# Row maxima in pieces, projections over 128 + 64 channels, a reordered end of each attention layer, and seven products whose results nobody reads

## The reference, cut to what matters

```python
y = layer_norm(x) * scale + bias                 # then padded to 28 x 28, windows of 14 x 14
q, k, v = split(windows(y) @ qkv_w + qkv_b)      # 12 heads of 16 channels
attn = einsum(q / 4, k) + rel_h(q) + rel_w(q)    # 196 x 196 per head and window
out = softmax(attn) @ v
x = x + unwindow(out @ proj_w + proj_b)
h = gelu(layer_norm(x) @ fc1_w + fc1_b)          # 192 -> 768
x = x + h @ fc2_w + fc2_b                        # 768 -> 192
```

## Time and profile before

| | us |
|---|---|
| median of 3 runs | 443.46 (442.67 to 444.38) |
| the profiled execution | 443.95 |
| its span, first to last instruction | 441.8 |
| TensorE busy in it | 385.9 (87%) |
| VectorE busy | 198.7 (45%) |
| ScalarE busy | 145.4 (33%) |
| GpSimd busy | 98.2 (22%) |
| mean granted TensorE clock | 0.973 |

### The profile page before, as it was taken

One profiled execution on the slowest core, in us unless ns is written; L12 is line 12 of the kernel. 1 busy time (PEld: TensorE's weight loads), 2 busy tenths in 40 slices (PEclk: granted clock), 3 DMA queues, 4 the chain that ended last, 5 costly groups with the idle time before them and its releaser, 6 DMA issues.

```text
span 441.8 us, 10357 instructions
## 1 busy us (share of the span) xinstructions
PE 385.9 (87%) x4462; PEld 279.3 (63%) x4462; DVE 198.7 (45%) x435; ACT 145.4 (33%) x314; POOL 98.2 (22%) x180
## 2 busy tenths in 40 slices
PE   5979877888776999999979987887879699999997
PEld 2468865556654447968737865555657254986657
DVE  6325555655647210225853455455555430151282
ACT  2462343343352151021156234434344034011220
POOL 2304057321225230000040407622123300000000
PEclk8899999999999799999999999999999699999999
DMA  7960000000020102000201000000000000000002
GB/s 212 274 163 5 2 2 5 2 4 2 4 83 2 45 0 56 34 20 1 71 3 25 1 4 3 4 2 3 4 3 1 1 0 1 0 1 0 0 1 71
DMA packets 8302, 12.32 MB, mean 28 GB/s; under 512 B 3041, under 2 KB 5922, under 8 KB 8258
## 3 DMA queue, kind: packets, MB, share of 16 engines
q1 hardware_dynamic: 8258, 11.68, 9.5%
HBM read 10.25 MB, written 0.79 MB: 25 GB/s over the span
## 4 chain that ended last, share of the span: by engine, by line
PE 69%; DVE 21%; ACT 5%; issue 2%; DMA 1%; SPq 1%
PE banks L824 9%; PE banks L728 9%; PE banks L833 7%; DVE negmax L1228 7%; PE banks L761 7%; PE banks L666 5%; PE banks L677 5%; DVE negmax L1232 4%; PE banks L654 3%; DVE o_turned L1247 3%; DVE inverse_sums L1253 3%; PE banks L686 3%; PE banks L748 2%; ACT o_and_sums L1063 2%; PE banks L993 2%
## 5 line engine op out<-in xcount | busy, mean ns | idle before, releaser
L1071 ACT ACTIVATE arena<-banks 128x392 f32<-128x392 f32 (+2 forms) x144 | 58.7, 494 | 71.4 <-PE banks L748 71.4
L824 PE MATMUL banks<-yT,fc 96*128 96x512 f32 x96 | 48.5, 660 | 4.7 <-ACT yT L1018 2.9
L1228 DVE TENSOR_REDUCE negmax<-banks 128x8 f32<-128x1568 f32 x24 | 42.4, 1765 | 18.5 <-PE banks L728 18.5
L606 POOL TENSOR_TENSOR attention_arena<-o_and_sums,inverse_sums 128x196 f32<-128x196 f32 (+2 forms) x36 | 19.6, 545 | 124.0 <-DVE inverse_sums L1253 124.0
L728 PE MATMUL banks<-attention_arena 32*128 32x196 f32 x384 | 28.6, 367 | 19.0 <-DVE negmax L1228 15.8
L1247 DVE STREAM_TRANSPOSE o_turned<-o_and_sums 128x224 f32<-128x224 f32 x36 | 14.8, 411 | 64.2 <-ACT o_and_sums L1063 64.1
L824 PEld LDWEIGHTS banks<-yT,fc 96*128 96x128 f32 x96 | 19.8, 213 | 29.3 <-issue 22.5
L761 PE MATMUL banks<-arena,v_and_ones 128*32 128x196 f32 (+2 forms) x672 | 30.9, 308 | 4.1 <-ACT arena L1071 4.1
L728 PEld LDWEIGHTS banks<-attention_arena 32*128 32x128 f32 x384 | 15.5, 183 | 29.3 <-DVE negmax L1228 20.2
L833 PEld LDWEIGHTS banks<-fc,arena 128*128 128x128 f32 x192 | 31.3, 190 | 1.0 <-issue 1.0
L833 PE MATMUL banks<-fc,arena 128*128 128x192 f32 x192 | 31.5, 326 | 0.0
(11 more groups left out here) (155 smaller groups left out, 636.6 us busy)
## 6 DMA issues: line engine op xcount, KB each, us to landing
fc<-in_fc SPq DMA_DIRECT2D x4, 576.0 KB, 6.2
attention_arena<-negmaxT SPq DMA_DIRECT2D x72, 1.0 KB
rel<-in_rel SPq DMA_DIRECT2D x2, 448.0 KB, 5.2
qkv<-in_qkv SPq DMA_DIRECT2D x2, 432.0 KB, 4.7
x_tok<-in_x SPq DMA_DIRECT2D x4, 192.0 KB, 3.4
inverse<-in_inverse SPq DMA_DIRECT2D x1, 768.0 KB
edge_rel<-negmaxT SPq DMA_DIRECT2D x48, 0.5 KB
inverse<-in_space_back SPq DMA_DIRECT2D x1, 768.0 KB, 4.4
```

The lines of the kernel that those rows point to most:

```text
L824: last = mm(m.bank[j % 4][:, :], wl["fc1"][:, half, 128 * hid:128 * (hid + 1)], m.yT[:, half, 512 * g:512 * (g + 1)], start=half == 0, sto ...
L1071: run(m.probsT[:, n % P_RING, j, 0:cols], m.bank[4 + j][:, 0:cols], ACT.Exp).then_inc(s.probs, 1)
L1228: dve.tensor_reduce(at[:, 0:8].rearrange("k (j a) -> k j a", a=2), m.banks[:, 0:4, 0:2 * MAIN_KEYS].rearrange("k j (a n) -> k j a n", a=2) ...
```

## The change

Line numbers of the changed kernel are higher: its `score` is L792, `turn` L812, `weigh` L825, `project` L707 and L713, values L726 and L732, `relate` L755, the products that nobody reads L740, fc1 L886, maxima L1305, ScalarE's tables L1083.

- **Layout.** `m.yT` and the weights hold channels 0 to 127 in one half and 64 to 191 in the other. A product over 192 channels is now one over 128 rows ("long") and one over 64 rows ("short"). Even jobs take the short one from partitions 64 to 127, odd jobs from 0 to 63, into different banks, and the short ones of a batch follow one another. `qkv` and `fc1` loads grow by a third.
- **Projections.** The jobs use all eight banks; v and v_edge come before rel_w and rel_h. The second `turn_norm` stands right in front of the product that waits for it. Results of the six c jobs come only after all six long products.
- **Maxima in pieces.** Each piece writes columns 0 to 195 of four banks and has its own TENSOR_REDUCE. The first five pieces alternate between banks 0 to 3 and 4 to 7, all in front of turn(0); later ones use banks 0 to 3. `AHEAD` is 2: iteration n is turn(n), the last piece of group n + 2, weigh(n - 1), the first piece of group n + 3 (edges have one piece). VectorE takes both maxima ahead of `invert(n - 1)`.
- **End.** fc1 uses eight banks in batches of four, long products first; the output of image 3 is projected between the long and the short ones of the first batch, into bank 7. ScalarE does two Gelus, loads the root's table, takes the second root, loads the Gelu table again. GpSimd's bias addition waits for six Gelus.
- **Products nobody reads.** `keep_warm` makes 128 x 512 products: 2 in front of rel_w, 3 in front of turn(0), 2 in front of the transposes of the end.

The diff, cut:

```diff
+PROJ += [("v", n, 0, "act") for n in range(IMAGES)] + [("v_edge", n, 0, "act") for n in range(2)]
 PROJ += [("rel_w", n, 0, "act") for n in range(SIDE // 2)] + [("rel_h", n, 0, "dve") for n in range(SIDE // 2)]
+def job_bank(j):
+    return (4 + j) % 8
...
-AHEAD = 3
+AHEAD = 2
...
+PIECES = [(n, part) for n, (_, b) in enumerate(GROUPS) for part in range(parts(b))]
+FIRST_PIECES = PIECES.index((AHEAD, 0)) + 1
+
+
+def piece_bank(i):
+
+    return 4 * (i % 2) if i < FIRST_PIECES else 0
+
+
+def max_before(i):
+
+    return i - 1 if i < FIRST_PIECES else i
...
+def out_bank(b):
+    return b if b < 2 else 4 + b
 
...
+                pool.wait_ge(s.fc1.act, HID_TILES)
...
+            def rest_rows(n):
+
+                return slice(REST, 128) if n % 2 == 0 else slice(0, REST)
+
+            def open_bank(s, j):
+
+                if j >= 8:
+                    wait_for(pe, s.proj_in, *taken_out(j - 8))
+                return m.bank[job_bank(j)]
+
+            def project(l, first, last):
+
                 s, wl = A[l], w[l]
...
+                for short in (False, True):
+                    for j in range(first, last):
+                        kind, g, part, _ = PROJ[j]
+                        bank = m.bank[job_bank(j)] if short else open_bank(s, j)
+                        rows = rest_rows(j) if short else slice(0, 128)
+                        if kind == "c":
+                            if not short and g == 0:
+                                if part == 1:
+                                    turn_norm(s.ln[0], 0, 1)
+                                pe.wait_ge(s.ln[0].act, part + 1)
+                                pe.wait_ge(s.ln[0].dve, part + 1)
+                            half = (j + short) % 2
+                            ins = mm(bank[:, :], wl["qkv"][rows, half, 128 * g:128 * (g + 1)], m.yT[rows, half, 512 * part:512 * (part + 1)],
+                                     start=not short, stop=short)
...
+                for pair in range(first, first + IMAGES, 2):
+                    for tile in range(2):
+                        for j in (pair, pair + 1):
+                            rows, at = rest_rows(j), 128 * (2 * (j - first) + tile)
+                            ins = mm(m.bank[job_bank(j)][:, CH * tile:CH * (tile + 1)], m.yT[rows, 1 - j % 2, at:at + 128],
+                                     wl["qkv"][rows, 1 - j % 2, 2 * CH:3 * CH], start=False, stop=True, skip_group_check=True)
+                            if tile == 1:
+                                ins.then_inc(s.proj_in.pe, 1)
+
+            def keep_warm(l, bank, n):
+
+                for _ in range(n):
+                    mm(m.bank[bank][:, :], m.yT[:, 0, 0:128], m.yT[:, 0, 0:512], start=True, stop=True)
+
...
+                if max_before(i) > 0:
+                    pe.wait_ge(s.max, max_before(i))
...
+                project(l, 0, 2 * CHUNKS)
+                project_values(l)
+                project(l, job("v_edge", 0, 0), job("v_edge", 1, 0) + 1)
+                wait_for(pe, s.proj_in, *taken_out(job("rel_w", 0, 0) - 8))
+                keep_warm(l, job_bank(job("rel_w", 0, 0)), 2)
+                for j in range(job("rel_w", 0, 0), len(PROJ)):
+                    relate(l, j)
+                for i in range(FIRST_PIECES):
+                    score(l, i)
 
                 pe.wait_ge(v_ones_set, 2)
+                wait_for(pe, s.proj_in, *taken_out(job("v_edge", 1, 0)))
+                pe.wait_ge(s.max, max(i for i in range(FIRST_PIECES) if piece_bank(i) == 4) + 1)
+                keep_warm(l, 7, 3)
                 for n in range(N_GROUPS):
                     turn(l, n)
-                    ahead = n + AHEAD
-                    if ahead < N_GROUPS:
-                        score(l, ahead, 0)
+                    if n + AHEAD < N_GROUPS:
+                        score(l, PIECES.index((n + AHEAD, parts(GROUPS[n + AHEAD][1]) - 1)))
                     if n > 0:
                         weigh(l, n - 1)
-                    if ahead < N_GROUPS:
-                        score(l, ahead, 1)
+                    if n + AHEAD + 1 < N_GROUPS and parts(GROUPS[n + AHEAD + 1][1]) == 2:
+                        score(l, PIECES.index((n + AHEAD + 1, 0)))
                     for b in range(2):
                         if n == OUT_AT[b] + 1:
                             if b == 0:
                                 pe.wait_ge(s.loaded["late"], 16 * 3)
-                                pe.wait_ge(s.max, N_GROUPS)
+                                pe.wait_ge(s.max, len(PIECES))
                             out_project(s, wl, b)
                 weigh(l, N_GROUPS - 1)
                 out_project(s, wl, 2)
+                keep_warm(l, 3, 2)
                 turn_norm(s.ln[1], 4, 0)
...
+                        if j == 0:
+                            pe.wait_ge(s.out_proj.dve, 2)
+                        elif j >= 8:
+                            pe.wait_ge(s.fc1.act, j - 7)
...
+                for first in range(0, 2 * HID_TILES, 4):
+                    for j in range(first, first + 4):
+                        if j == HID_TILES:
+                            turn_norm(s.ln[1], 4, 1)
+                        fc1(j, False)
+                    if first == 0:
+                        pe.wait_ge(s.pv_out, N_GROUPS)
                         out_project(s, wl, IMAGES - 1)
+                    for j in range(first, first + 4):
+                        fc1(j, True)
...
-                root(s.ln[1], 1)
                 load_table(ACT.Gelu)
                 for j in range(2 * HID_TILES):
                     g, hid = divmod(j, HID_TILES)
                     if j == 2:
+                        load_table(ACT.Sqrt, 1)
+                        root(s.ln[1], 1)
+                        load_table(ACT.Gelu, 2)
+                    if j == 4:
                         take_norm(wl, s.ln[1], 4, 9, 1)
                     act.wait_ge(s.fc1.pe, j + 1)
...
+                        dve.tensor_reduce(at[:, 0:8].rearrange("k (j a) -> k a j", a=2)[:, part], m.banks[:, bank0:bank0 + 4, 0:MAIN_KEYS],
+                                          AX, ALU.max, negate=True).then_inc(s.max, 1)
...
+                for i in range(FIRST_PIECES):
+                    take_max(i)
+                    if n + AHEAD < N_GROUPS:
+                        take_max(PIECES.index((n + AHEAD, parts(GROUPS[n + AHEAD][1]) - 1)))
+                    if n + AHEAD + 1 < N_GROUPS and parts(GROUPS[n + AHEAD + 1][1]) == 2:
+                        take_max(PIECES.index((n + AHEAD + 1, 0)))
                         invert(n - 1)
-                    if n + AHEAD < N_GROUPS:
-                        take_max(n + AHEAD)
...
+def _split(v):
+
+    return np.stack([v[:128], v[REST:]], 1)
...
+        out[f"qkv{l}"] = _split(np.concatenate(chunks(qw, kw) + [vw], 1))
+        out[f"fc1{l}"] = _split(g("fc1_w"))
```

More of the change, by code:

```diff
@@ new lines, in project_values @@
+            def project_values(l):
+                s, wl = A[l], w[l]
+                first = job("v", 0, 0)
+                for j in range(first, first + IMAGES):
+                    bank = open_bank(s, j)
+                    for tile in range(2):
+                        at = 128 * (2 * (j - first) + tile)
+                        mm(bank[:, CH * tile:CH * (tile + 1)], m.yT[:, j % 2, at:at + 128], wl["qkv"][:, j % 2, 2 * CH:3 * CH],
+                           start=tile == 0, stop=False, skip_group_check=True)
+                for pair in range(first, first + IMAGES, 2):
[5 more added lines that the diff above has]
+                            if tile == 1:
+                                ins.then_inc(s.proj_in.pe, 1)
```

197 lines of the change are left out of this document (81 added, 116 removed).

## The result

| | kernel before | kernel after |
|---|---|---|
| median, us | 443.92 (442.67 to 444.43) | 414.06 (413.48 to 414.58) |
| profiled execution, us | 443.95 | 413.48 |
| its span, us | 441.8 | 411.6 |

The ratio is 0.933, with a 95% interval of 0.931 to 0.936: 29.9 us faster. The forecast was 415.5 with a range of 407 to 426. Its three terms came out less well than their sum.

What follows compares the result with a forecast made beforehand. TensorE's waits for VectorE's maxima were taken as the main bound, then the layers' end and the start. Savings of 18.5 (loop), 1.4 (start) and 8.5 (end), 28.4 in all, gave 415.5 us; forecast 411 to 420, wider range 407 to 426.

Steps and rivals of the forecast that it cites:

- The loop: The group loop of both attention layers, turn(0) to turn(16): 64.8 us against 74.05, 9.2 us less in each layer.
- ring of 7.9 us: Edge iterations 6 to 10: piece, maximum, transpose, four transfers and turn take 7.9 us over two iterations, 5 x 4.0 = 20.
- full window: Loop iterations 0 to 4 and 12 to 14, with two pieces each: a period of 4.05 us, 8 x 4.05 = 32.4.
- what is late next is TensorE itself: In the loop after the change, TensorE (3.8 us a period) was to be the next limit, with VectorE as close.
- The end: End of each attention layer, normalising and fc1: 4.3 us less a layer, 8.5 less in both.
- gap in front of product 6: In fc1, a new TensorE wait of about 4 us behind Gelus, table loads and root; clock falls there, costing 2.2.
- The start: From the c jobs to turn(0): 0.6 us less in one layer, 2.0 in the other, 1.2 for the clock: 1.4 less.
- short products don't overlap: Rival, chance 0.12: pairs of 64-row products don't run at once, costing 19 us in all: 434 us.
- transfers decide: Rival, chance 0.14: transfers of row maxima in edge iterations need more than 3.4 us, 7 to 8 in all: 423 us.
- the clock never falls: Rival, chance 0.12: unread products hold the clock where falls were expected, 3.2 x 2 and 1.2 less: 408 us.
- table loads cost more than their row: Rival, chance 0.03: each of two loads in fc1's gap holds ScalarE twice its 1.28 us, 5.1 in all: 421 us.
- it is slower: Rival, chance 0.03: short products neither overlap nor hide their weight loads, 22 us more on top of 434: 456 us.

Runs made afterwards that it cites:

- same_rows: The kernel after with every short product of 64 rows in the same rows 64 to 127 of the array: 429.54 us, ratio 0.970.
- root_early: The kernel after with the second root back in front of the Gelu table load, two table loads fewer in each fc1: 410.67 us, ratio 0.926.
- half_max: The kernel after with each piece's maximum taken over 98 of its 196 columns, part of the computation left out: 405.01 us, ratio 0.916.

## Why the prediction was right, and where it wasn't

**What bounds the kernel before** was read rightly: the part of the maximum that turn does not cover in the loop, and the end's low clock and table load.

**The loop** was 1.5 us a layer too good. Edge iterations took 19.93 (I had 20), iteration 11 5.14 (5.0), one-piece iterations 3.68 (3.7). The 20 was luck: I had a ring of 7.9 us over two iterations through the transfers, and said that turn would wait for nothing else there. It waits for them in two of ten, and in the others turn, piece and weigh on TensorE, with ScalarE's exponentials beside them and its copy behind both, make 3.9 to 4.1. What failed is the full window: 4.24 for 4.05, eight times, which is the whole of it. Two terms of it were mis-sized. The maximum of 784 inputs takes 0.97, not 0.92: the slope of 1.09 ns between the rows of 1568 and 1280 inputs leaves a fixed part of 0.06 us, where it is some 0.16 (0.567 for 392 inputs, 0.974 for 784). And the first piece takes 0.94, not 0.84, as it too starts behind a wait: its first batch takes 0.43 (55.74 to 56.17), one in a row 0.33 (58.63 to 58.96). With both, the maxima and not TensorE close the ring, so "what is late next is TensorE itself" named the wrong one of two that lie 0.47 us apart. VectorE's inverse sums are done at 56.68 and the maximum starts at 56.83: not late, as forecast.

**The end** was 2.9 us too poor over both layers. I let the clock fall in the gap in front of product 6 every time (2.2), and half the time at the start of fc1 (1.0 a layer). In seven profiles with this order of ScalarE's and the same gap the clock fell in 7 of the 14 gaps, and cost 1.4 to 1.7 (24.13 to 22.43); in the shorter gaps of same_rows and root_early it fell in none. At the start of fc1 it fell in all six cases of the old end and in none of 18 with the new one and its two unread products; without these it fell in one of four. fc1 at full clock is 22.43, not 21.5: product 6 came where I had it (12.98 for 12.9), and what follows it took 9.45 for 8.6, mostly by changes of rows that the sum had at nothing (below). It starts 1.35 earlier (1.1); normalising took 1.34 us, less than the 1.6 I took (it was 2.69).

**The start** was near by chance. Forecast: 3.0 later at rel, 3.6 back before turn(0), with 0.6 and 2.0 less and 1.2 for the clock. In the second layer c to rel came 4.3 later (18.35 for 14.03), not 3.0. My own terms add up to 3.2 (15.9 against 12.7), and to 3.4 with the larger load. Beyond that 0.5 is that the transposes wait for the normalisation there (from the first c product to the fourth it takes 5.25, and 4.72 in the first layer), and most of the rest are terms taken short (edges 1.36 for 1.1, unread products 1.9 for 1.7, short value products 1.5 for 1.4). rel to the first score took 1.4 less (11.36 for 12.74), as no clock fell (the idle time in front of rel had been 2.37 us in both layers of the kernel before, not 1.65, and the clock had fallen in one), and from there to turn(0) 3.5 less (7.95 for 11.41). That sums to 0.5 less, not 2.0. In the first layer turn(0) came 3.5 us earlier in one profile and 2.0 in the other of the same kernel, and within 0.1 to 0.3 of before in two kernels that share its start.

**The rivals.** That short products don't overlap: refuted by same_rows. That transfers decide: two waits of 0.7. That the clock never falls: half true. That table loads cost more than their row: refuted, 1.28 and 1.28 in the gap, as I had them. That it is slower: refuted. Of the unread products I had the two prices right (1.7 for the first pair, measured 1.9; 1.1 for the three, measured 1.1 and 1.2), and that they fill no wait in front of rel.

So the gain was put 3.0 too high in the loop, 2.9 too low at the end, 2.6 too low at the start in this profile, and 0.8 too high outside. The sum is good because they cancel, which is luck.

**The changes of rows.** I had put a change of the rows at 0.10 us and left it out of the sum. The traces show its price. The same 28 records of 512 columns, one after another, in the kernel before and in same_rows:

```profile
157.95 12.18 PE L824 MATMUL banks<-yT,fc 96*128 96x512 f32 x28
```

```profile
347.42 12.87 PE L886 MATMUL banks<-yT,fc 128*128 128x512 f32 x28 [1.22 <-ACT yT L1092]
```

In a row a record starts 0.43 us after the one before. At each of the three changes between 128 and 64 rows in the second stretch one step is 0.52 and the next 0.53, 0.2 us together, and its first step is 0.53 too, behind a wait. Where the rows change between 96 and 128, in the kernel before, no step is longer. The kernel after has twelve such changes a layer, with the same steps (0.09 and 0.10 over those in a row): 24 x 0.19 = 4.6 us of TensorE's time, of which 0.6 us a layer are in the 9.45 behind product 6, and 1.2 a layer in front of rel. In the sum they stood at nothing; the 2.4 us in all that the prediction left in its range are half of this. The Trainium skill, "TensorEngine Tiling (Array Packing)", Key Properties, says that a change of the tiling mode drains TensorE. The traces agree, with 0.19 us for each change.

## What to carry to other kernels

When two engines take turns on the same buffers, write the ring down with what each hand-over adds (a batch behind a wait, the fixed part of the other engine's instruction) before asking which engine has more work: here the ring of 4.24 beat TensorE's 3.8. Filler work has to be looked at in the trace for what it stands in front of; five of seven unread products here delayed the next work by 3.1 us a layer, and no fall of the clock was seen without them. Small products that pair up pay for each switch to them and back: put them in few batches. And a load that is moved forward moves another back: name which.

## What the runs showed of the hardware

- Two products of 64 rows in opposite halves of the array run at once: 16 records of 192 columns in 1.57 us, against 2.86 in the same half.
- A batch of products behind a semaphore wait takes 0.43 us where the same batch in a row takes 0.33; its weight loads start with it (0.31 for eight, the first line of the period above). In half_max the piece behind weigh, which waits for nothing, also has 0.43 for its first batch (the piece behind turn has not), so a change of the tile's shape costs this too.
- A change between products of 128 rows and of 64 rows costs TensorE 0.19 us, 24 times in the kernel after; one between 96 and 128 rows costs nothing that the trace of the kernel before shows.
- A maximum over four banks costs 0.567 us for 392 inputs, 0.974 for 784 and 1.765 for 1568: about 1.03 ns each and 0.16 fixed.
- Four `normed` of 128 x 192 take 2.69 us on VectorE while GpSimd's additions run beside them, and 1.34 where GpSimd is idle for most of it; why is not shown.
- After the same idle time the granted clock falls in some executions and not in others: behind the gap of 3.5 us (2.2 of it idle, the rest transposes) in 7 of 14 cases. At the start of the program it varied from no fall to 0.51 from 8.5 to 15.5, in kernels with the same instructions there, and the start of rel lay between 26.61 and 30.76.
